# One VectorE pass moved behind another, and half of a product of ones replaced by a VectorE addition, in a one-core decoder layer

## The reference: one decoder layer over 16 batches

```python
x = _layernorm(x + attn(x, Wq, bq, ..., Ao))          # 16 heads of 32, LoRA of rank 16
x = _layernorm(x + xattn(x, ctx, ctx, decay))         # r = decay * r + k * v; out = q * r
x = _layernorm(x + ffn(x, w1, b1, ln_g, ln_b, w2, b2))
# attn: softmax(q k^T / sqrt(32)) v, then the output projection
# ffn: h = layer_norm(gelu(silu(bitlinear(x, w1, b1)))) * ln_g + ln_b; bitlinear(h, w2, b2)
# bitlinear: rows rms-normed and rounded to 127 steps of their maximum, weights ternary
```

## Time and profile before

| what | value |
|---|---|
| median of 3 runs | 1053.55 us (1053.01 to 1054.15) |
| the profiled execution's own time | 1050.57 us |
| its span | 1048.7 us |
| TensorE busy | 945.9 us, 90% |
| VectorE busy | 907.5 us, 87% |
| ScalarE busy | 827.6 us, 79% |
| GpSimd busy | 605.9 us, 58% |
| mean granted TensorE clock | 0.96 of full |

### The profile page before, as it was taken

How to read it: one execution, slowest core, us unless ns; L and a number is a source line. 1 busy time by engine, 2 the same in 40 slices (tenths; PEclk the granted TensorE clock), 3 DMA queues, 4 the chain that set the end, 5 groups by cost and what they waited for, 6 DMA issues and landing times.

```text
span 1048.7 us, 23313 instructions
## 1 busy us (share of the span) xinstructions
PE 945.9 (90%) x9260; PEld 650.5 (62%) x9260; DVE 907.5 (87%) x1490; ACT 827.6 (79%) x957; POOL 605.9 (58%) x767
## 2 busy tenths in 40 slices
PE   5998997999999999999999999999999999977515
PEld 3866756676677767676767766676767676644202
DVE  4678878999998999999999989999999999995766
ACT  3646686888979797988879897979888888977684
POOL 2332337474756759485756658494857576572643
PEclk9998998999999999999999999999999999988668
DMA  9432200223122121323131221323131321112213
GB/s 360 154 119 104 73 2 21 74 52 84 22 75 61 48 68 52 84 52 84 48 88 21 60 69 39 83 52 84 52 84 23 93 41 54 44 49 64 52 33 89
DMA packets 106352, 73.67 MB, mean 70 GB/s; under 512 B 91386, under 2 KB 91386, under 8 KB 104451
## 3 DMA queue, kind: packets, MB, share of 16 engines
q1 hardware_dynamic: 105522, 70.34, 24.4%
q10 hardware_dynamic: 720, 1.84, 0.5%
HBM read 41.73 MB, written 8.40 MB: 48 GB/s over the span
## 4 chain that ended last, share of the span: by engine, by line
DVE 34%; PE 28%; ACT 15%; issue 9%; POOL 7%; DMA 7%; SPq 1%; DVEq 0%; ACTq 0%; POOLq 0%
PE bank L1484 11%; PE bank L1345 7%; DVE neg_max L964 6%; DVE h L1095 6%; POOL h L549 5%; DMA xqT<-xq 5%; DVE stats L1021 3%; ACT h L725 3%; ACT junk L735 3%; ACT h L740 3%; PE bank L1485 3%; DVE fz L1100 2%; DVE qk_parts L987 2%; DVE rows L1037 2%; ACT L725 2%
## 5 line engine op out<-in xcount | busy, mean ns | idle before, releaser
L964 DVE TENSOR_REDUCE neg_max<-wave 128x8 f32<-128x2048 f32 x64 | 146.1, 2283 | 19.2 <-PE wave L1370 19.1
L549 POOL TENSOR_TENSOR h<-h,g_tile 128x2048 f32<-128x2048 f32 x30 | 139.4, 4645 | 39.1 <-ACT h L740 39.1
L657 ACT ACTIVATE probs<-wave 128x1024 f32<-128x1024 f32 x128 | 124.4, 1024 | 35.9 <-PE wave L1394 35.7
L1484 PE MATMUL bank<-w,xqT 128*128 128x512 fp8e4 x496 | 130.1, 386 | 23.7 <-DMA xqT<-xq 23.7
L439 POOL TENSOR_SCALAR attn_hi<-attn 128x256 fp32r<-128x256 f32 x64 | 30.2, 473 | 148.6 <-DVE attn L1003 132.9
L695 ACT ACTIVATE rows<-rows,rstd 128x512 f32<-128x512 f32 x96 | 74.3, 807 | 41.7 <-POOL rstd L455 23.8
L719 ACT ACTIVATE h<-bank,qx 128x512 f32<-128x512 f32 x124 | 83.9, 689 | 25.4 <-PE bank L1485 23.2
L1095 DVE TENSOR_TENSOR h<-h,b_tile 128x2048 f32<-128x2048 f32 x32 | 83.9, 2623 | 18.2 <-POOL h L549 18.1
L1484 PEld LDWEIGHTS bank<-w,xqT 128*128 128x128 bf16 x496 | 47.8, 99 | 81.4 <-issue 20.8
L1491 PE MATMUL bank<-w,hqT 128*128 128x512 fp8e4 x416 | 94.3, 380 | 0.2 <-DMA hqT<-h 0.2
L498 POOL TENSOR_TENSOR rows<-rows,bo_tile 128x512 f32<-128x512 f32 x32 | 51.6, 1633 | 71.1 <-DMA rows<-x 71.1
(11 more groups left out here) (184 smaller groups left out, 2841.9 us busy)
## 6 DMA issues: line engine op xcount, KB each, us to landing
ctx_sb<-ctxT SPq DMA_DIRECT2D x16, 512.0 KB, 3.7
rows<-x SPq DMA_DIRECT2D x16, 512.0 KB, 4.0
out<-rows SPq DMA_DIRECT2D x32, 256.0 KB, 2.5
xT_in<-xT SPq DMA_DIRECT2D x15, 512.0 KB, 4.7
h<-w1T SPq DMA_DIRECT2D x4, 1024.0 KB, 14.8
h<-w2T SPq DMA_DIRECT2D x4, 1024.0 KB, 4.9
h<-Wq SPq DMA_DIRECT2D x1, 1024.0 KB, 6.1
h<-Wk SPq DMA_DIRECT2D x1, 1024.0 KB, 9.7
```

Of the source, the lines that this page charges most:

```text
L549: po.tensor_tensor(h_of(b, q)[:, :], h_of(b, q)[:, :], g_tile[:, :], ALU.mult).then_inc(done, 1)
L657: ac.activation(probs[:, kt, :, :], wave[:, :, kt * T:(kt + 1) * T], ACT.Exp, scale=SM_SCALE).then_inc(S["probs_ready"], 1)
L964: dv.tensor_reduce(neg_max[:, :, :], wave[:, :, :].rearrange("p j (t k) -> p j t k", t=NT), axis=AX_X, op=ALU.max, negate=True).then_inc(S ...
L1484: pe.matmul(p[:, :], xqT[:, q, kc, :], w1[:, kc, n * FW:(n + 1) * FW], start=(kc == 0), stop=False)
```

## The change

Three things are changed. On VectorE the second ln_b pass, `z_add(j-2, 1)`, stands behind `quantise_x(j-1)` instead of ahead of it, and on ScalarE the square that reads it, `z_square(j-2, 1)`, stands ahead of `zq_store` instead of ahead of `xq_store`. For group 3 VectorE adds the key halves in place, into `probs[:, 1]`, after the value product has read them, and TensorE's product of ones for that group, now four matmuls, stands behind the q/k product of group 1 of batch j+1 (`summed`).

```diff
--- before.py
+++ after.py
@@ -160,7 +160,7 @@
         table = [
 
             (PE, "shifted_ready", 4), (PE, "scores_ready", 4), (PE, "qk_ready", 4), (PE, "v_ready", 2),
-            (PE, "shiftT_ready", 4), (PE, "pv_ready", 4), (PE, "o_ready", 2), (PE, "rT_ready", 2),
+            (PE, "shiftT_ready", 4), (PE, "pv_ready", 4), (PE, "values_ready", 1), (PE, "o_ready", 2), (PE, "rT_ready", 2),
             (PE, "f_ready", 8), (PE, "y_ready", 2),
 
             (AC, "probs_ready", 8), (AC, "v_stored", 2), (AC, "x_hi", 1), (AC, "qk_hi", 8),
@@ -169,7 +169,7 @@
             (AC, "xq_stored", 1), (AC, "silu_done", 8), (AC, "zq_stored", 2),
             (AC, "gelu_done", 2), (AC, "h_var", 2), (AC, "h_normed", 2), (AC, "z_squared", 2),
 
-            (DV, "half_added", 1), (DV, "qk_lo", 8), (DV, "max_done", 4), (DV, "shift_split", 8), (DV, "inverted", 12), (DV, "attn_done", 4),
+            (DV, "half_added", 2), (DV, "qk_lo", 8), (DV, "max_done", 4), (DV, "shift_split", 8), (DV, "inverted", 12), (DV, "attn_done", 4),
             (DV, "scan_done", 5), (DV, "ln1", 6), (DV, "ln2", 6), (DV, "x_quant", 14),
             (DV, "z_added", 4), (DV, "z_quant", 12),
             (DV, "ln3", 6),
@@ -864,8 +864,6 @@
                     v_store(j + 1, 0)
                 if alive(j, 0):
                     probs_of(j, 3)
-                if alive(j, 2):
-                    z_square(j - 2, 1)
                 if alive(j, 1):
                     xq_store(j - 1)
                 if alive(j, -1):
@@ -875,6 +873,7 @@
                 if alive(j, 0):
                     ctx_square(j)
                 if alive(j, 2):
+                    z_square(j - 2, 1)
                     zq_store(j - 2, 0)
                 if j == 1:
                     ternary_store(7)
@@ -979,6 +978,13 @@
                 wait(dv, "xq_stored", b - 2, 1)
                 dv.tensor_tensor(half_sum, probs[:, 0, :, :], probs[:, 1, :, :], ALU.add).then_inc(S["half_added"], 1)
 
+            def add_in_place(b):
+
+                wait(dv, "probs_ready", b, 8)
+                wait(dv, "values_ready", b, 1)
+                dv.tensor_tensor(probs[:, 1, :, :], probs[:, 0, :, :], probs[:, 1, :, :],
+                                 ALU.add).then_inc(S["half_added"], 1)
+
             def qk_lo(b, c):
 
                 wait(dv, "qk_hi", b, 2 * (c + 1))
@@ -1215,6 +1221,7 @@
                 attn_norm(0, 2)
                 ternary(1)
                 maxima(1, 0)
+                add_in_place(0)
                 attn_norm(0, 3)
                 qk_lo(1, 1)
                 ternary(2)
@@ -1262,10 +1269,11 @@
                     qk_lo(j + 1, 0)
                 if alive(j, 0):
                     attn_norm(j, 2)
-                if alive(j, 2):
-                    z_add(j - 2, 1)
                 if alive(j, 1):
                     quantise_x(j - 1)
+                if alive(j, 2):
+                    z_add(j - 2, 1)
+                add_in_place(j)
                 if alive(j, 2):
                     quantise_z(j - 2, 0)
                 if j == 1:
@@ -1405,17 +1413,26 @@
                 for kt in range(NT):
                     for i in range(GH):
                         ch = (GH * c + i) * HD
-                        pe.matmul(bank[4][i * HD:(i + 1) * HD, 0:T], v_sb[b % 2][:, kt, ch:ch + HD], probs[:, kt, i, :],
-                                  start=(kt == 0), stop=(kt == NT - 1))
-                if c == 0:
-                    wait(pe, "half_added", b, 1)
+                        last = pe.matmul(bank[4][i * HD:(i + 1) * HD, 0:T], v_sb[b % 2][:, kt, ch:ch + HD],
+                                         probs[:, kt, i, :], start=(kt == 0), stop=(kt == NT - 1))
+                if c == 3:
+                    last.then_inc(S["values_ready"], 1)
+                else:
+                    summed(b, c)
+
+            def summed(b, c):
+
+                if c in (0, 3):
+                    wait(pe, "half_added", b, 1 if c == 0 else 2)
+                    both = half_sum if c == 0 else probs[:, 1, :, :]
                     for i in range(GH):
-                        last = pe.matmul(bank[4][i * HD:(i + 1) * HD, T:2 * T], ones[:, :], half_sum[:, i, :],
+                        last = pe.matmul(bank[4][i * HD:(i + 1) * HD, T:2 * T], ones[:, :], both[:, i, :],
                                          start=True, stop=True)
-                for kt in range(NT if c > 0 else 0):
-                    for i in range(GH):
-                        last = pe.matmul(bank[4][i * HD:(i + 1) * HD, T:2 * T], ones[:, :], probs[:, kt, i, :],
-                                         start=(kt == 0), stop=(kt == NT - 1))
+                else:
+                    for kt in range(NT):
+                        for i in range(GH):
+                            last = pe.matmul(bank[4][i * HD:(i + 1) * HD, T:2 * T], ones[:, :], probs[:, kt, i, :],
+                                             start=(kt == 0), stop=(kt == NT - 1))
                 last.then_inc(S["pv_ready"], 1)
 
 
@@ -1602,6 +1619,7 @@
                 scores(1, 0)
                 weighted(0, 3)
                 qk(1, 1)
+                summed(0, 3)
                 shiftT(1, 0)
                 shifted(1, 0)
 
@@ -1665,6 +1683,7 @@
                     weighted(j, 3)
                 if alive(j, -1):
                     qk(j + 1, 1)
+                summed(j, 3)
                 if j == 1:
                     pe.wait_ge(u_tern, 4)
                     pe.wait_ge(u_b1_in, 16 * NPART)
```

More of the change, by code:

```diff
@@ L1264, in body @@
                     attn_norm(j, 2)
+                if alive(j, 1):
+                    quantise_x(j - 1)
                 if alive(j, 2):
                     z_add(j - 2, 1)
-                if alive(j, 1):
-                    quantise_x(j - 1)
+                add_in_place(j)
                 if alive(j, 2):
```

## The result

The changed kernel takes **1061.35 us** (median of five runs, 1060.23 to 1064.65) where the kernel before took 1054.15 beside it (1053.01 to 1055.45). The ratio is 1.0076, interval 1.0057 to 1.0095, so it is slower by 6 to 10 us. The forecast was 1064.4, with a range of 1056 to 1069.

A forecast was written before the change was run, and what follows sets the result against it. Bound: a chain of waits through VectorE, with TensorE nearly full. Fourth f product 0.77 us later plus 0.12 over 11 periods gives +9.8; with the other batches and lead +10.9 on 1053.55, so 1064.4 us, range 1056 to 1069.

The forecast's parts named there:

- The slack of 0.38 us: Ahead of the fourth f product on TensorE: the first silu allows it at T+6.37, it runs at T+6.75.
- The collision: `quantise_x`'s two-column instruction on VectorE against GpSimd's `attn_lo`: between 0.43 gain and 0.24 loss, taken as 0.12 us loss.
- the lucky case: `quantise_x`'s two-column instruction slips in ahead of GpSimd's `attn_lo` and takes 0.17 us, a gain of 0.43.
- the prediction's sentence on that rule: By the rule alone, `attn_hi` also holds the small `tensor_tensor` in `quantise_x`: loss 0.24 instead of 0.12, sum 1.3 us higher.
- j=2: Batch 2: fourth f product, held by the silu, goes from T+6.85 to T+7.64, +0.8 us.
- j=15: Batch 15: fourth f product, not held by the silu, moves from T+8.46 to about T+7.5, -0.9 us.
- j=1: Batch 1: `attn_norm` and maxima wait for the later product of ones, delaying the shift's transpose; +0.7 us (0 to 1.5).
- The lead: Ahead of the periods: `qk_lo(1, 1)` stands behind `attn_norm(0, 3)`, which waits for the later ones; +0.4 us (0 to 1.2).
- TensorE as the bound: Rival: TensorE or its wait for xqT bounds the kernel, so the change is faster, 1047 us; 6%.
- Slower by little: Rival: `quantise_x`'s two-column instruction starts ahead of `attn_lo`, leaving 0.34 us a period, 1058.4 us; 15%.
- The path over the maxima: `maxima(j+1, 0)` has its shift at T+7.58 instead of T+6.43; its transpose, behind the fourth f product, at T+7.83: covered.
- the rival N: Rival in the experiments' expectations: later `attn_norm(j, 3)` and `maxima(j+1, 0)` cost, not the silu; moving the addition later leaves 1061; no chance given.

The follow-up runs named there:

- mid silu: The changed kernel with ScalarE's `zq_store` of block 0 moved from ahead of the table load to between the first and second silu; 1049.43 us, ratio 0.9968.
- the pass alone: The kernel before with only the second ln_b pass moved behind `quantise_x`, and its square with it; 1044.07 us, ratio 0.9913.
- no addition: The changed kernel without group 3's half additions, all 16 matmuls of its product of ones behind the q/k product; 1051.55 us, ratio 0.9986.
- late addition: The changed kernel with the in-place addition moved behind `quantise_z(j-2, 0)`, directly ahead of `attn_norm(j, 3)`; 1060.52 us, ratio 1.0068.
- the fastest kernel: The kernel before with only the ln_b pass and its square moved, and `zq_store` of block 0 between first and second silu; 1040.80 us, ratio 0.9891.
- ln_b with the early silu: The kernel before with only the ln_b pass and its square moved, and `zq_store` of block 0 behind the first four silus; 1114.02 us, ratio 1.0582.
- early silu: The changed kernel with `zq_store` of block 0 moved from ahead of the first silu's table load to behind the first four silus; 1116.01 us, ratio 1.0438.

## Why the prediction was right

**The mechanism held in each step.** The wait for xqT is gone, a wait for silu ahead of the fourth f product has come (1.25 us, forecast 1.4), `zq_store` waits 1.35 instead of 0.41, and the period of 58.68 lies in the forecast 58.6 to 58.9. Counted from T as the prediction has it (the issue of the transpose plus 2.20), the fourth product starts at 788.65 - 781.14 = T+7.51, forecast T+7.52. The experiment that takes the silu off the addition, and nothing else (mid silu), takes 1.1 us off the period again.

**The slack of 0.38 us** came from one row of batch 2, and it was the term on which the sign hung. It holds: from first silu to fourth product it is 788.65 - 787.91 = 0.74 in the change, so before the silu allowed 12.60 + 0.74 = 13.34 where the product stood at 13.71, a slack of 0.37. With the pass alone the product moved up until it met the silu (13.16).

**The collision** was mis-sized, with an end that hardly differs, by luck. I took +0.12 at the two-column instruction (line 1072 now); here it took 0.17, the lucky case, and the `tensor_tensor` two further on took 0.40. GpSimd and VectorE in the change, then the same two lines with their fates exchanged, in no addition:

```profile
774.55 0.19 POOL L556 TENSOR_SCALAR fs<-fs 128x1 f32<-128x1 f32 x1
...
775.85 0.74 POOL L442 TENSOR_TENSOR attn_lo<-attn,attn_hi 128x256 fp32r<-128x256 f32 x1
```

```profile
775.81 0.17 DVE L1072 TENSOR_SCALAR qx<-qx 128x2 f32<-128x2 f32 x1
...
776.21 0.40 DVE L1074 TENSOR_TENSOR qx<-qx 128x2 f32<-128x2 f32 x1
```

```profile
767.83 0.62 DVE L1072 TENSOR_SCALAR qx<-qx 128x2 f32<-128x2 f32 x1
...
768.68 0.16 DVE L1074 TENSOR_TENSOR qx<-qx 128x2 f32<-128x2 f32 x1
```

So `quantise_x` is 0.18 us shorter than before, not 0.12 longer. In exchange the way from the fourth f product back to the next slot is 0.21 longer (44.38 against 44.17), for which I had no term. 0.77 - 0.18 + 0.21 = 0.80 is the period's measured difference; the forecast had 0.89. Two errors of 0.30 and 0.21 us nearly cancel.

The 0.21 is GpSimd's line 534, which every period passes. In the change it starts while VectorE's half addition of group 0 (line 979) still runs and ends with it, after 0.39 us; where the addition is over it takes 0.19. All other steps of that way are the same to 0.03 us. VectorE and GpSimd in the change, then GpSimd before:

```profile
746.18 1.21 DVE L979 TENSOR_TENSOR x_round<-probs 128x1024 f32<-128x1024 f32 x1
```

```profile
747.04 0.39 POOL L534 TENSOR_SCALAR fs<-fs 128x1 f32<-128x1 f32 x1 [1.03 <-ACT junk L735]
```

```profile
794.53 0.19 POOL L534 TENSOR_SCALAR fs<-fs 128x1 f32<-128x1 f32 x1 [1.29 <-ACT junk L735]
```

It is not the same in all changed kernels: with a late addition or the mid silu line 534 takes 0.19 in nearly every period, without the addition 0.33 to 0.99. Before it took 0.19 in five of eleven periods and up to 0.39 in the others, so that there too some periods are 58.0 and more.

The Trainium skill ("SBUF — State Buffer", "Who interferes with whom") has VectorE's instructions with two SBUF inputs exclude GpSimd's that read SBUF, the later of the two waiting for the whole of the other. The 0.40 of the small `tensor_tensor` beside `attn_lo`, the 0.39 of line 534 and the 4.19 beside `g_mul` agree. The `tensor_tensor` that the prediction's sentence on that rule spoke of, now line 1071, took 0.17 in the middle periods of the change although it lay beside `attn_hi`; there the rows show no hold.

**The ends.** j=2: fourth product at T+7.52, +0.67 against +0.8. j=15: T+7.50 instead of T+8.46, -0.96 against -0.9. j=1: the shift is transposed 1.04 us later after its T (138.05 - 127.06 against 134.58 - 124.63), against +0.7. The lead, +0.4, can't be told.

**The total.** From the transpose of j=2 to that of j=15 the profile of after is 9.5 us longer (762.9 against 753.4), the forecast for that stretch 10.7. In whole the forecast added 10.9 us, the two profiled executions lie 12.2 apart, and the medians 7.2 (6 to 10). So the forecast increase is somewhat too large against the medians, by the 0.09 a period and by something that the one profile of each kernel cannot show. That 1050.57 + 10.9 = 1061.5 meets the measured median is luck: the sum belongs on a median, and there it gives 1064.4.

**The rivals.** TensorE as the bound (6%) is wrong for this change, but close one step further: in the fastest kernel it is busy 56.6 of 57.0 us, and the fourth f product waits for nothing. "Slower by little" had the lucky collision right and its price wrong, since the next instruction paid. The path over the maxima I had named and called covered, which it is as long as the fourth f product is late. In the late addition my theory left it out, and only the rival N had it: moving the addition away from the silu leaves it ahead of the maxima.

## What to carry to other kernels

A pass taken off the head of an engine's queue gives back only the slack of the next chain in line, so look for an instruction further back that waits for the same engine over a third one: here 1.15 us of new work on VectorE went through a store and a table load on ScalarE to TensorE. Where a long chain passes through an in-order engine, see whether the consumer that isn't urgent (`zq_store`, 2.00 us) stands ahead of the urgent one; moving it behind one instruction gained 12 us, moving it behind four lost 55 by the medians (38 by the ratios). Before relying on a move, find the place where two paths meet and work out for each of them what it would give as a period; in this kernel the silu's, the maxima's and TensorE's lie within 1.7 us (58.68, 57.56 and 57.0).

## What the runs showed of the hardware

- TensorE's clock fell after two gaps of 1.15 and 1.25 us with one f product between them in some periods (four matmuls 1.76 us instead of 1.04) and not in others, with the same gaps. After one gap of 2.81 us, in ln_b with the early silu, the sixteen matmuls of y still took 3.61 us, as after gaps of 1.6; after one of 2.11 in the early silu they took 5.30. The length of a gap did not tell by itself what the clock would do.
- A small instruction took many times its length by its place beside one of the other engine: VectorE's 128x8 `tensor_tensor` 4.19 us instead of 0.18 beside GpSimd's 4.5 us product, GpSimd's 128x1 `tensor_scalar` 0.40 instead of 0.19 beside VectorE's half addition, in nearly every period of the change and on the path that sets it.
- A two-column instruction of VectorE took 0.17 or 0.62 us by its place beside GpSimd's, and the wait moved to a neighbour (0.16 or 0.40) when it was spared.
- The table load of 1.28 us doesn't wait for the silu's input: in mid silu it began at 773.86, ahead of the first f product's matmuls, and the silu then waited 0.53 us. Where ScalarE comes to it in time it lies beside TensorE's work; behind `zq_store`, as in the change, all of it is on the path.
- Two kernels with the same lead, some 125 us of it, differed there by 3.3 us between their profiled executions.
